# A hybrid layer kernel: the C gate made on VectorE from the PSUM bank, in place of a ScalarE copy and a GpSimd product

## What is computed

```
x_and_res = x @ Wi + bi;  xs = silu(first half);  res = second half
x_dbl = xs @ Wx + bx                 # d_raw (64), B_sel (64), C_sel (256)
delta = softplus(d_raw @ Wdt + bdt);  A = -exp(A_log)
h[t] = exp(delta[t] * A) * h[t-1] + delta[t] * B[t] * xs[t]      # per channel and state
y[t] = C[t] * sum over states of h[t]
out  = ((y + xs * Dp) * silu(res)) @ Wo + bo
```

## Time and profile before

| what | value |
| --- | --- |
| median of 3 runs | 1849.11 us |
| lowest and highest of them | 1846.08 and 1857.18 us |
| the profiled execution's own time | 1861.63 us |
| its span in the trace | 1859.7 us |
| DVE busy, POOL busy | 1514.5 us and 1513.9 us |
| ACT busy, PE busy | 1281.5 us and 1351.0 us |

### The profile page before, as it was taken

The page is one execution under the profiler, slowest core; times in us unless marked ns, Lnnn a source line. Parts: engine busy times, 40 slices in busy tenths (PEclk is TensorE's granted clock), DMA queues, the critical chain, the costliest instruction groups (busy, mean ns, idle before and its releaser), DMA issues.

```text
span 1859.7 us, 19053 instructions
## 1 busy us (share of the span) xinstructions
PE 1351.0 (73%) x5928; PEld 617.7 (33%) x5928; DVE 1514.5 (81%) x2105; ACT 1281.5 (69%) x2275; POOL 1513.9 (81%) x888
## 2 busy tenths in 40 slices
PE   4336458777886887778776878778787778668958
PEld 1001123234342343324342343324332343324535
DVE  4879988898889889898899888888888988895222
ACT  4547668687877778777777778777787777755423
POOL 0899999978998799977998899987998799983312
PEclk9557569889987989879897989879898898979979
DMA  3601411122111311132101401132111321100000
GB/s 87 212 34 71 164 46 51 49 91 97 57 40 48 148 51 33 54 104 96 55 25 50 162 29 51 49 106 81 51 51 49 102 85 52 46 29 1 7 1 6
DMA packets 38747, 121.89 MB, mean 66 GB/s; under 512 B 5875, under 2 KB 21110, under 8 KB 26358
## 3 DMA queue, kind: packets, MB, share of 16 engines
q1 hardware_dynamic: 37062, 120.67, 18.3%
q10 hardware_dynamic: 1584, 0.01, 0.0%
HBM read 109.13 MB, written 11.53 MB: 65 GB/s over the span
## 4 chain that ended last, share of the span: by engine, by line
PE 27%; ACT 18%; DVE 15%; POOL 14%; issue 8%; DVEq 0%; POOLq 0%; ACTq 0%
DVE h L1251 10%; POOL w L947 9%; PE bankH L565 8%; ACT da L837 5%; PE bankY L579 5%; PE bankG L565 5%; ACT yk L798 4%; ACT L837 3%; PE ys L633 2%; POOL x L890 2%; PE bankG L512 2%; DVE aq L1189 1%; PE bankY L559 1%; ACT L785 1%; ACT sq L785 1%
## 5 line engine op out<-in xcount | busy, mean ns | idle before, releaser
L1251 DVE TENSOR_TENSOR_SCAN h<-da,w 128x512 f32<-128x512 f32 x1024 | 1192.1, 1206 | 158.3 <-ACT da L837 133.0
L947 POOL TENSOR_TENSOR w<-ur,br 128x1024 f32<-128x1024 f32 x512 | 1193.6, 2365 | 33.1 <-DVE h L1251 21.2
L837 ACT ACTIVATE da<-dr,al 128x511 f32<-128x511 f32 x1024 | 681.9, 687 | 221.9 <-DVE h L1251 212.5
L633 PE MATMUL ys<-h,wsum 128*32 128x512 f32 x2048 | 320.9, 703 | 208.5 <-DVE h L1251 189.2
L565 PE MATMUL bankH<-nT,w 128*128 128x512 f32 x512 | 301.8, 673 | 89.7 <-DVE aq L1189 85.3
L890 POOL TENSOR_TENSOR x<-x,yk 128x512 f32<-128x512 f32 x128 | 163.1, 1274 | 211.2 <-ACT yk L798 210.6
L579 PEld LDWEIGHTS bankY<-w,aq 128*128 128x128 f32 x2048 | 262.8, 203 | 87.0 <-issue 65.0
L579 PE MATMUL bankY<-w,aq 128*128 128x128 f32 x2048 | 270.5, 289 | 12.4 <-DVE aq L1189 7.9
L565 PE MATMUL bankG<-nT,w 128*128 128x512 f32 x432 | 243.8, 648 | 24.6 <-DVE aq L1189 24.6
L798 ACT ACTIVATE yk<-bankY,rt 128x128 f32<-128x128 f32 x512 | 151.8, 364 | 121.5 <-PE bankY L579 107.8
L633 PEld LDWEIGHTS ys<-h,wsum 128*32 128x32 f32 x2048 | 42.9, 115 | 408.5 <-DVE h L1251 373.2
(11 more groups left out here) (187 smaller groups left out, 1135.8 us busy)
## 6 DMA issues: line engine op xcount, KB each, us to landing
br<-b_rows SPq DMA_DIRECT2D x64, 1024.0 KB, 5.0
dr<-d_rows SPq DMA_DIRECT2D x16, 1024.0 KB, 7.1
ur<-u_rows SPq DMA_DIRECT2D x16, 1024.0 KB, 8.4
d_rows<-vh SPq DMA_DIRECT2D x16, 256.0 KB
u_rows<-th SPq DMA_DIRECT2D x16, 256.0 KB
xnew<-in_L_attn_a_x_dram SPq DMA_DIRECT2D x8, 256.0 KB, 5.3
w<-in_L_ffn_W_dram SPq DMA_DIRECT2D x2, 1024.0 KB, 11.1
x<-in_L_attn_a_x_dram SPq DMA_DIRECT2D x8, 256.0 KB, 9.1
```

The source lines that it names most:

```text
L633: ins = nc.tensor.matmul(ys[32 * q:32 * q + 32, :], wsum[:, :], h[:, (DUOS * t.b + 2 * group + q // 2) % H_RING, q % 2, :], start=(n == 0) ...
L837: A(da[duo % D_RING][:, k % 2, 1:L], dr[:, half, q, 1:L], ACT.Exp, scale=nega[:, QUADS * half + q, n:n + 1]).then_inc(decay_ready, 1)
L947: G.tensor_tensor(w[:, turn_duo % W_RING, :, :], ur[:, half, q:q + 2, :], br[:, chunk % B_RING, row:row + 1, :].to_broadcast([128, 2, L]), ...
L1251: V.tensor_tensor_scan(h[:, turn_duo % H_RING, k % 2, :], da[duo % D_RING][:, k % 2, :], w[:, turn_duo % W_RING, k % 2, :], 0.0, ALU.mult, ...
```

## The change

DVE makes the gate in one `scalar_tensor_tensor`: (bank + bias) * `sres`, written to `cg`, which counts the bank as drained. It stands at slot 83+2 = 85 for C0 and 85+3 = 88 for C1 (`GATE_LAGS`), for the first batch behind its setup. `cg` gets two buffers, for even and odd batches. ACT's copy, POOL's product, the tile `cm` and the semaphores `gate_ready` and `c_ready` are left out, with the waits on them.

```diff
+GATE_LAGS = (2, 3)
...
-        steps_and_b = sb("steps_and_b", [128, L]); cm = sb("cm", [128, 2, L])
+        steps_and_b = sb("steps_and_b", [128, L])
-        cg = sb("cg", [128, 2, L]); xd = sb("xd", [128, 2, L]); resa = sb("resa", [128, TT, D])
+        cg = sb("cg", [128, 2, 2, L]); xd = sb("xd", [128, 2, L]); resa = sb("resa", [128, TT, D])
...
# ScalarE, pre_a
-                def gates():
-                    for m in range(2):
-                        yield t.slot(f"C{m}") + ACT_LAG
-                        if m == 0 and not known(i, 1):
-                            act.wait_ge(gate_ready, 2 * i)
-                        copy_out(t, f"C{m}", cm[:, m, :], None, ACT.Identity, bias=bxc[:, m:m + 1])
...
# GpSimd, gates
-                    yield GATES_AT + 3 + 3 * half
-                    if half == 0:
-                        if not known(b, 1):
-                            pool.wait_ge(ys_taken, 2 * b)
-                        pool.wait_ge(c_ready, b + 1)
-                    G.tensor_tensor(cg[:, half, :], cm[:, half, :], sres[:, half, :], ALU.mult).then_inc(gate_ready, 1)
...
# VectorE, pre_a
-                        v.wait_ge(gate_ready, 2 * i)
...
+                def gates():
+                    for m in range(2):
+                        yield t.slot(f"C{m}") + GATE_LAGS[m]
+                        for n in range(2, 4):
+                            v.wait_ge(drained[BANK[f"in{n}"]], t.before(f"in{n}") + 1)
+                        p = got(t, f"C{m}")
+                        drain(f"C{m}", V.scalar_tensor_tensor(cg[:, i % 2, m, :], p[:, :], bxc[:, m:m + 1], sres[:, m, :], ALU.add, ALU.mult))
...
-                v.sem_inc(c_ready, 1)
...
# VectorE, take_sums
-                v.wait_ge(gate_ready, 2 * b + half + 1)
-                V.tensor_tensor(y3[:, half, :], ys[:, :], cg[:, half, :], ALU.mult).then_inc(ys_taken, 1)
+                V.tensor_tensor(y3[:, half, :], ys[:, :], cg[:, b % 2, half, :], ALU.mult).then_inc(ys_taken, 1)
```

More of the change, by code:

```diff
@@ L287, in hybrid_kernel @@
         scanned = sem("scanned"); summed = sem("summed"); ys_taken = sem("ys_taken")
-        gate_ready = sem("gate_ready"); skip_ready = sem("skip_ready"); direct_ready = sem("direct_ready"); c_ready = sem("c_ready"); res_ready = sem("res_ready")
+        skip_ready = sem("skip_ready"); direct_ready = sem("direct_ready"); res_ready = sem("res_ready")
         stats_ready = [sem(f"stats_ready{k}") for k in range(5)]; moments_ready = [sem(f"moments_ready{k}") for k in range(5)]
@@ L766, in pre_a @@
                     act.preload_act_table_set(DECAYS)
-                    yield from gates()
                 else:
@@ L1115, in pre_a, with steps @@
                     drain(f"in{m}", V.scalar_tensor_tensor(dst, th[:, m % 2, :], 1.0, banks[BANK[f"in{m}"]][:, :], ALU.add, ALU.mult))
-                for m in range(2):
-                    yield t.slot("dt1") + 6 + m
-                    v.wait_ge(relu_ready, 2 * i + m + 1)
-                    v.wait_ge(log_ready, i + 1)
-                    drain(f"dt{m}", V.tensor_tensor(dl[:, m, :], spa[:, m, :], banks[BANK[f"dt{m}"]][:, :], ALU.add))
-                if known(i, 1):
-                    yield t.slot("C1") + 5
+                def steps():
+                    for m in range(2):
+                        yield t.slot("dt1") + 6 + m
+                        v.wait_ge(relu_ready, 2 * i + m + 1)
+                        v.wait_ge(log_ready, i + 1)
+                        drain(f"dt{m}", V.tensor_tensor(dl[:, m, :], spa[:, m, :], banks[BANK[f"dt{m}"]][:, :], ALU.add))
+                def gates():
+                    for m in range(2):
+                        yield t.slot(f"C{m}") + GATE_LAGS[m]
[3 more added lines that the diff above has]
+                        drain(f"C{m}", V.scalar_tensor_tensor(cg[:, i % 2, m, :], p[:, :], bxc[:, m:m + 1], sres[:, m, :], ALU.add, ALU.mult))
+                if known(i, 1):
+                    yield from steps()
+                    yield from gates()
+                else:
+                    yield from gates()
+                    yield from steps()
                 for m in range(2):
                     v.wait_ge(drained[BANK[f"C{m}"]], t.before(f"C{m}") + 1)
-                v.sem_inc(c_ready, 1)
             def take_sums(b, half, t, at):
```

## The result

Measured beside each other on one chip, the changed kernel took 1862.96 us (median of 12 runs, 1858.84 to 1868.33) and the kernel before 1853.69 (12 runs, 1846.08 to 1858.04). The ratio is 1.0054, with a 95% interval of 1.0038 to 1.0069. So the change costs 9.3 us. The forecast was 5.5 us less than before, and its range ended at 1859. It was wrong in sign and out of its range. Of the 19.4 us between 1843.6 and 1862.96, 4.6 lie in the starting value: the median before was 1849.11 over 3 runs and is 1853.69 over 12.

The account below looks back on a forecast made before the run. DVE and POOL, each busy 81% of the span, were taken to bound the kernel. POOL's relief less C1's gate summed to -5.5 us, from 1849.11 to 1843.6 us, with an 8-in-10 range of 1830 to 1859.

Parts of the forecast that it names:

- What goes from POOL: Two products a turn leave POOL's queue, 1.22 us each; worth 1.0 us a turn at slot 78, 2.4 in turn 0.
- the first product: POOL's gate product at 713.00 in turn 3: worth 0, its sum then waiting 1.62 us for `yk` instead of 0.40.
- slots 52 and 56: DVE scans in turn 3: slot 52's 0.73 us of idle brings nothing, slot 56's 0.71 us goes.
- slot 78: DVE's moments, which wait 1.88 us for POOL's expert sum: gain between 0.71 and 1.22 us, taken as 1.0.
- Turn 0: No expert sum to wait for, so both POOL products count and DVE's gaps absorb its gates: -2.4 us.
- What goes from ACT: Two copies a turn of 0.69 us leave ACT; taken as 0, or 11 us with all 16 on the path.
- C0's gate: On DVE behind slot 85's scan: a 1.7 us stop uses up idle ahead of the first S5 step; cost 0.
- C1's gate: On DVE behind the S5 scan of 788.74: no wait, but 0.65 us a turn where DVE has no gap.
- The rule on SBUF inputs: DVE instructions with two SBUF inputs and GpSimd SBUF reads block each other; the bias column was judged not to count.
- gates held: Rival: DVE gates held behind POOL products, half a product each 1860 us, a whole product 1877; chance 0.03.
- The sum: Turn 0 -2.4, turns 1 to 6 -2.1, turn 7 -1.0: together -5.5 us, to 1843.6 us; forecast chance 0.45.
- The clock rival: Small moves shift where clock stretches fall: 1840.7 us if turn 2 shortens, 1858.1 if five others lengthen; chance 0.25.

Follow-up runs that it names:

- after_no_dve_gate: Changed kernel with both gates off DVE, ACT copying the C banks into `cg`, no POOL product, silu(res) factor left out: 1846.65 us, ratio 0.9983.
- the twelve waits filled: Zero-weight dummy matmuls ahead of twelve PE waits: before 1825.14 us, changed 1817.46, changed with C1's gate by ACT's copy and POOL's product 1823.83.
- after_c1_on_act: Changed kernel with half 1's gate written by ACT's copy, its silu(res) left out, only the C0 gate on DVE: 1847.77 us, ratio 0.9990.
- nine places: Zero-weight dummy matmuls ahead of nine PE waits in each scan turn: kernel before 1834.10 us, changed kernel 1827.12.
- after_fill_more: Changed kernel with zero-weight dummy matmuls ahead of twelve PE waits: 1817.46 us, ratio 0.9814 to the kernel before.
- before_dummy_short: Kernel before plus a half-width (256 columns) DVE dummy with one PSUM operand, slot 88, turns 1 to 6, DVE waiting for it: 1862.19 us.
- before_dummy: Kernel before plus one DVE dummy at slot 88 in turns 1 to 6, all operands in SBUF, behind the S5 scan: 1864.88 us, ratio 1.0066.
- before_dummy_bank: Kernel before plus one DVE dummy with the gate's kinds of operands, ahead of slot 88's S5 scan, turns 1 to 6: 1869.57 us, ratio 1.0111.

## Why the prediction was wrong, point by point

- **What goes from POOL.** Right up to slot 56: no gain from the first product (the wait for `yk` grew to 1.61), slots 52 and 56 without a wait. Wrong at slot 78: the wait there was to get shorter and stayed at 1.88 (1.93 in turn 3). The working let `yk` move ahead with DVE. In after_no_dve_gate, where POOL's relief stands alone, `yk` did not move: in turn 3 it was complete 128.4 us behind the scan of slot 0, as before, POOL waited 1.33 us for it, and turns 2 to 6 are 0.1 us shorter than the common turn before, where 1.0 was forecast. Turn 0, forecast at -2.4, went from 167.05 to 165.99 us, and to 167.03 with the products put back. All in all the relief is worth 4.8 to 6.7 us in the changed kernel (forecast 1.0 x 7 + 2.4 = 9.4) and, for the second product alone with the twelve waits filled, 6.4 plus whatever the C1 gate costs there (1817.46 against 1823.83).
- **What goes from ACT.** Nothing spoke against 0; no run has that part alone.
- **C0's gate.** Right: a stop of 1.73 us, no wait at the S5 step, cost 0 (after_c1_on_act).
- **C1's gate.** Right in place and in its 0.65 us of queue time. Wrong in price: I put a delay on a chain down at its own length, 0.65 x 6 = 3.9 us. It goes with low stretches at other places; the changed kernel without it is some 15 us faster (1862.25 against 1847.77 in one job), and delays of 0.49 to 0.64 us put into the kernel before cost 11.8 and 19.2 us.
- **The rule on SBUF inputs.** The gate kept its 0.72 to 0.75 us beside POOL's products, so here the bias column doesn't count as a second SBUF input. The rival "gates held" fell.
- **The sum.** With PE's waits filled its total comes near: -7.0 us with nine places, -7.7 with twelve, against -5.5. That isn't a test at a fixed clock, since the clock still falls in most turns there, and POOL's term, as above, did not come out by itself in the plain kernel. The step that failed is the one behind the sum, that it can be taken off the median of a kernel whose turns differ by 3 us with the clock: the runs gave +9.3 us. Of turns 2 to 6 of the profiled executions two were long before (214.9 us) and three after (214.5 to 215.0), and the short ones went from 211.7 to 212.3 us, not to 211.4.
- **The clock rival.** It was named, with its mechanism and with 1858.1 as its bad end. I gave it 0.25, and bounded it by "the five others become as long as turn 2". The earlier trace rows showed that the clock decides 2.9 us a turn, more than any term of the sum (-1.0, +0.65). That row should have made this the likeliest case, with a direction left open and a range to about 1870. "Nothing says which way" was true; it argued for a wider range, not for a small chance.
- **The profile pair hid part of it.** The profiled executions differ by 2.4 us (1861.63 and 1864.06), the medians by 9.3. The one of before, at 1861.63, is slower than all its 12 timed runs, which lie between 1846.08 and 1858.04. It holds two turns of the long kind (214.9 us). That many of its other runs have fewer of them fits their higher mean clock, but no trace of such a run was kept.

What stays open: why the pattern settles where it does. The runs show that turns prefer a few lengths and that small delays choose between them. They don't give a rule that tells which delay leads to which. That the placing of the low stretches is the whole of the loss isn't shown either; the turned sign with fillers, and the kernels with equal work and different turns, say that it is most of it.

## What to carry to other kernels

Where the same stretch of code shows two granted clocks in one trace, compare what they cost DVE with the change you price: if that is more than the change's own terms, time the change also with PE's waits filled, or its sign means little. Fill the waits of PE that stand ahead of matmuls which the bounding engine needs, look at the granted clock behind each, and then price the move of work between engines again. A control at other waits belongs with it, since dummies can cost as much as they gain.

## What the runs showed of the hardware that I had not expected

- Turns settle on few lengths. Without fillers turns 2 to 6 took 211.6 to 212.3 or 213.8 to 215.5 us in nearly all kernels, the changed one and the one before alike. With nine or more places filled many took about 208.2, others 205.7 to 211.7; the shortest, 205.7, is turn 4 of after_fill_more, which has no stretch of 1.2 GHz. The three commonest lengths, 208.2, 211.6 and 215.0, lie equally far apart. A saving of 1 us can vanish in such a turn (211.7 to 211.6 in after_no_dve_gate), and a delay of 0.49 us can cost 2 us a turn (before_dummy_short).
- A wait of PE of the same 2.88 us was followed by 2.4 GHz in one kernel and by 1.2 GHz in the other. In the 70 matmul records before it PE did the same, at the same spacing; its place in time was not the same. "TensorE: Matmul & The Clock Gate", Part 1 of the Trainium skill, says that the window in which activity is judged runs freely and isn't reset when a kernel starts. These rows agree with that.
- An instruction of DVE with both tensors in SBUF was stretched beside POOL's products. Four of the six dummies in before_dummy started while a product of POOL was under way; each ended 0.55 us behind that product and took 1.37 to 1.82 us. The other two, one with no product beside it and one that started as a product ended, took 0.72. The shortest, median and longest:

```profile
L1118 DVE SCALAR_TENSOR_TENSOR y<-y,bxc x6: 723/1544/1822, 355.8 to 1424.1; 128x512 f32<-128x512 f32 x6
```

  With one tensor in PSUM the same form took 0.726 us (before_dummy_bank). "SBUF — State Buffer" of the Trainium skill, section "Who interferes with whom", says that two SBUF inputs contend with a GpSimd instruction that reads SBUF. The six dummies agree, and so do the ten gates beside a product, which have one tensor in SBUF and took 0.75 us at most.
